# A graph layer on one core: each gather signals the landing of the tile four places back, not seven

## What is computed

```python
k = _decomp(x, nt, w_comp_k, w_basis_k).reshape(n, H, DK)     # q and v likewise
kt = jnp.einsum('nhi,thij->tnhj', k, relation_att)[edge_type, src]
e = (q[dst] * kt).sum(-1) * relation_pri[edge_type] * scale
m = jax.ops.segment_max(e, dst, num_segments=n)
ex = jnp.exp(e - m[dst])
a = ex / jax.ops.segment_sum(ex, dst, num_segments=n)[dst]
vt = jnp.einsum('nhi,thij->tnhj', v, relation_msg)[edge_type, src]
agg = jax.ops.segment_sum(a[..., None] * vt, dst, num_segments=n).reshape(n, DH)
out = relu(_decomp(agg, nt, w_comp_a, w_basis_a) + x @ loop_weight + bias)
result = _layernorm(x + out)
```

## Time and profile before

| | us |
|---|---|
| median of 3 runs (1296.33 to 1299.81) | 1298.27 |
| profiled execution, its span | 1757.2 |
| first gather starts, last gather starts | 199.15, 1641.63 |
| first product on DVE, last | 266.3, 1663.7 |
| busy: PE, DVE, POOL, ACT | 1160.7, 986.6, 881.5, 785.6 |

### The profile page before, as it was taken

How to read it: one execution, slowest core, us unless ns; L and a number is a source line. 1 busy time by engine, 2 the same in 40 slices (tenths; PEclk the granted TensorE clock), 3 DMA queues, 4 the chain that set the end, 5 groups by cost and what they waited for, 6 DMA issues and landing times.

```text
span 1757.2 us, 31429 instructions
## 1 busy us (share of the span) xinstructions
PE 1160.7 (66%) x6730; PEld 962.9 (55%) x6730; DVE 986.6 (56%) x2832; ACT 785.6 (45%) x2217; POOL 881.5 (50%) x915
## 2 busy tenths in 40 slices
PE   8989875657556565566566655566565666656698
PEld 5445434656545554455455554565455565545587
DVE  7877463555445555445555554455554566545677
ACT  4667454444434434443344343443444354434324
POOL 2775354555555554545454545455545554545233
PEclk9999997777677767876777667766777687777699
DMA  8878754555555555545455555555555555555675
GB/s 261 323 289 316 284 172 140 157 148 158 152 159 153 157 151 151 149 141 151 150 163 148 158 152 154 148 160 164 151 162 154 154 168 148 155 150 162 187 242 194
DMA packets 225149, 309.08 MB, mean 176 GB/s; under 512 B 32423, under 2 KB 191119, under 8 KB 217781
## 3 DMA queue, kind: packets, MB, share of 16 engines
q1 hardware_dynamic: 159996, 188.75, 30.6%
q0 software_dynamic: 38880, 106.25, 23.4%
q10 hardware_dynamic: 26088, 12.08, 2.4%
HBM read 139.52 MB, written 58.78 MB: 113 GB/s over the span
## 4 chain that ended last, share of the span: by engine, by line
SPq 34%; issue 31%; PE 12%; DVE 9%; another core or an unknown queue 7%; DMA 2%; DVEq 2%; ACT 1%; POOL 1%; POOLq 0%; ACTq 0%
SPq L1173 27%; PE pb L1900 4%; SPq L1152 2%; PE pb L1923 2%; DVE agg L845 2%; SPq L481 2%; SPq L1170 2%; DVEq L814 2%; DMA kv<-ring 2%; PE pb L2084 1%; SPq L1168 1%; PE pb L2190 1%; PE pb L2028 1%; DVE kv L541 1%
## 5 line engine op out<-in xcount | busy, mean ns | idle before, releaser
L1458 POOL DMA_INDIRECT ring<-table,rows_idx x782 | 745.8, 954 | 736.6 <-SPq L1168 452.5
L2084 PE MATMUL pb<-work,onehot 128*128 128x136 f32 x1664 | 367.5, 358 | 214.1 <-DVE agg L845 152.8
L845 DVE TENSOR_TENSOR agg<-agg,pb 128x136 f32 x832 | 241.8, 291 | 459.9 <-remote 291.8
L2084 PEld LDWEIGHTS pb<-work,onehot 128*128 128x128 f32 x1664 | 307.0, 254 | 242.0 <-issue 210.9
L1650 ACT ACTIVATE work<-pb 128x512 f32<-128x512 f32 x208 | 124.0, 596 | 549.6 <-remote 376.2
L2028 PE MATMUL pb<-q_all,work 128*128 x1664 | 301.0, 340 | 1.3 <-issue 0.8
L2028 PEld LDWEIGHTS pb<-q_all,work 128*128 128x128 f32 x1664 | 280.6, 253 | 7.6 <-issue 4.9
L1637 ACT ACTIVATE work<-lane,neg_lane 128x128 f32<-128x128 f32 x800 | 253.3, 390 | 0.6
L2012 PE MATMUL pb<-ident,onehot 128*128 128x128 f32 x832 | 174.5, 347 | 115.6 <-issue 60.2
L2012 PEld LDWEIGHTS pb<-ident,onehot 128*128 128x128 f32 x832 | 125.4, 180 | 136.0 <-issue 71.3
L686 DVE TENSOR_TENSOR kv<-kv,pb 128x512 f32<-128x512 f32 x208 | 141.5, 680 | 96.6 <-issue 41.7
(11 more groups left out here) (239 smaller groups left out, 1237.2 us busy)
## 6 DMA issues: line engine op xcount, KB each, us to landing
kv<-ring SPq DMA_DIRECT2D x832, 128.0 KB
table<-kv SPq DMA_DIRECT2D x49, 1024.0 KB, 5.2
ring<-table,rows_idx POOLq DMA_INDIRECT x782
kv<-base_rows SPq DMA_DIRECT2D x7, 448.0 KB, 7.6
kv<-in_x_dram SPq DMA_DIRECT2D x8, 384.0 KB, 5.8
seg<-item_bias ACTq DMA_DIRECT2D x48, 64.0 KB
base_rows<-pair ACTq DMA_DIRECT2D x24, 128.0 KB
onehot<-coef_rows SPq DMA_DIRECT2D x3, 1024.0 KB, 5.5
```

The costliest lines, as they stand in the source:

```text
L845: v.tensor_tensor(a, a, PB[banks[i // 2 % len(banks)]][:, (i % 2) * 256:(i % 2) * 256 + W], ALU.add).then_inc(s_added, 1)
L1458: pool.indirect_dma_start(out=ring[:, o:o + 2 * D], out_offset=None, in_=table, in_offset=bass.IndirectOffsetOnAxis(ap=rows_idx[:, t:t + 1 ...
L2084: mm = t_.matmul(PB[banks[k % len(banks)]][:, u * 256:u * 256 + W], onehot[:, o:o + P], wv[:, b % WR, h * 2 + u, :], start=True, stop=True)
```

## The change

The constant AHEAD goes from 7 to 4. It has two uses: the tile that iteration t waits for and announces, and the number of tiles that are announced behind the loop.

```diff
@@ -87,7 +87,7 @@
     REAL = -(-E // P)
     RING = 16
-    AHEAD = 7
+    AHEAD = 4
     TSEMS = 8
     assert AHEAD < TSEMS and RING & (RING - 1) == 0 and GROUPS * G < ITEMS
```

## The result

The changed kernel is slower: median 1345.34 us of 4 runs (1340.1 to 1349.36) against 1298.7 us of the kernel before, ratio 1.0354 with a 95% interval of 1.0322 to 1.0387. The forecast was no change, with a range up to 1318 us.

The account below looks back on a forecast made before the run. The prediction took GpSimd's row of gathers, at 1.254 us each, to bound the timed kernel. From 1298.3 us it took 3 us of gain and added 3 us of cost, giving 1298 us, no change, range 1284 to 1318 us.

Parts of the forecast that it names:

- The bound: Whole timed kernel: GpSimd's row of gathers, 1.254 us each, sets the time, with PE close behind.
- the floor of 1282 to 1294 us: Time of a kernel whose GpSimd never waits; the median stood 4 to 16 us above it.
- Signals come earlier where GpSimd was held: GpSimd's freed wait: landed tiles are announced sooner, loosening the ring; 3 us gain taken, bounds 0 to 16 us.
- rival A: Freed wait, line 1455: the ring was too tight, so the change is faster, about 9 us, 1289 us; chance 0.21.
- The sequencer's lead shrinks: GpSimd's landing wait: gather t can't be handed over before tile t-4 is signalled; 3 us cost, bounds 0 to 39 us.
- limit (3.8 us): Longest time from a gather's start to its signal that delays no even gather; odd ones were allowed 4.3 us.
- rival B: Landing wait before even gathers: landings too late for four in flight; up to 39 us slower, 1318 us at half; chance 0.19.
- The share of late landings: Even gathers at the landing wait: one in twenty late by 0.15 us, 3 us in all.
- The upper bound, 39 us: Most the landing waits could cost: every sixth even gather late by 0.6 us.
- The page's rule: HBM access of 0.2 us on average, 2 us at high load; for the gathers some 300 us cost, given 1 in 100.
- Rival C: PE paces the groups and a cushion in ring and kv hides cost and gain: 1298 us; forecast with C 0.60.
- What the profile after would show: Signs: unheld gathers keep 0.30 us gaps, line 1168 waits stay GpSimd's largest (350 to 550 us), span within 2%.

Follow-up runs that it names:

- the second profile: The kernel before, unchanged, profiled a second time: span 1299.3 us in an execution of 1301.56 us.
- half_rows7: The kernel before (AHEAD = 7) with gathers of 512 bytes instead of 1 KB and copies halved from the third group on: 1279.84 us, ratio 0.9811.
- limit4_signal7: Against the kernel before: iteration t waits for tile t-4's landing but still announces only tile t-7: 1349.73 us, ratio 1.0386.
- load_twice7: The kernel before (AHEAD = 7) with the count load repeated in even iterations; the build dropped the repeat, leaving the same kernel: 1298.89 us, ratio 1.0008.
- two_counts4: The changed kernel (AHEAD = 4) with a second count load and freed wait in even iterations, behind the landing wait: 1393.01 us, ratio 1.0695 to the kernel before.
- half_rows4: The changed kernel (AHEAD = 4) with gathers of 512 bytes instead of 1 KB and copies halved from the third group on: 1298.03 us, ratio 0.9944 to the kernel before.

## Why the prediction was wrong

*The bound.* Right in substance. A row of gathers at 1.254 us paces the timed kernel: the second profile has a mean step of 1.270 us, and half_rows7, with half the bytes, has the pace of 1.254 us itself: 979.3 us for 781 steps, and no wait before a gather is longer than the fixed gap:

```profile
POOL ring L1460 <- issue: 218.4, 717, 0.3
```

It came to 1279.8 us, 2 us under the floor of 1282 to 1294 us, and its tail (105.1 us against 113.9) is shorter as well. The margin to the copies is small, though. The chain of the second profile runs through SyncE's copies more than through the gathers:

```profile
DMA kv<-ring 36%; SPq L1173 10%; DMA ring<-table,rows_idx 8%; PE pb L1900 6%; PE pb L1980 3%; PE pb L1923 3%; POOL ring L1458 3%; PE pb L2190 1%; POOLq L1452 1%; DVE kv L541 1%; DVE agg L845 1%; DVEq L814 1%; PE pb L1909 1%; DVE q_all L954 1%; PE pb L1969 1%
```

On line 1168 SyncE waits 142.2 us for its own copies there, yet it holds the gathers up by 6 us only. After the change the chain runs through the gathers' landings (34%, in the page shown with the result). One statement of this part is refuted: that recording stretches this program by a third. The second profile isn't stretched, and none of the twelve others is.

*Signals come earlier where GpSimd was held: 0 to 3 us of gain.* Not contradicted. limit4_signal7 leaves room for some microseconds, all behind the last gather and none in the row. Before the change only 6 us of GpSimd's waiting on SyncE were left, not 452.5. The 2.0 us of SyncE's waiting for signals, which bounded this term and spoke against rival A, were of the stretched execution: the second profile has 32.9 us, and the changed kernel 158.4.

*The sequencer's lead shrinks: 3 us of cost.* **This is the step that failed.** It measured some 58 us in the row of gathers and 46 us in the time. Mechanism, place and limit (3.8 us) were the right ones and stood there as rival B; the term was mis-sized by a factor of 15. The waits that B asked for are there, and longer than its 0.2 to 0.9 us: up to 2.4 us. Three errors are in it:

1. The share of late landings. I took one in twenty by 0.15 us, from two rows in the tail of the earlier trace rows; it was 114 of 383 by 0.65 us. Those rows came from the first and the last gathers of an execution in which SyncE's slowness kept the copies apart. I had worked out that the timed load is 0.77 in place of 0.52, which the second profile confirms to the digit, and then took the delays of a thinner stretch for it.
2. The upper bound, 39 us, was no bound. It counted late even gathers only and took the worst of twelve rows as the worst there is; the worst of 766 was 6.54 us. It also left out GpSimd's own pauses, below, 10.5 us of the 58.
3. A choice near the end that did no harm, where the evidence (one even row late in six) pointed at the other.

*The page's rule* of 2 us for a memory access at high load (the Trainium skill, DMA: Bandwidth & Descriptors, Latency and other measured facts) is supported in its direction: the median rose by 0.9 us from half to full rows, the 95% point from 4.05 to 4.97 us. No run shows the memory access by itself. Its far end, 1.8 us on every gather, is refuted: its 300 us were six times too much.

*Rival C, PE as the bound with a cushion,* fails. PE's 1.10 us a gather, 87% of the pace, came from the stretched execution, where the granted clock was 0.73. In the second profile the clock is 0.86 and PE is busy 594.6 us for 618 gathers, 0.96 us each, or 77%. And DVE waited for the copies into kv even before, and waits longer now:

```profile
DVE kv L686 <- DMA kv<-ring: 97.5, 75, 3.5
```
```profile
DVE kv L686 <- DMA kv<-ring: 146.7, 90, 3.8
```

(before, second profile; then after). There is no cushion: of the 58 us lost in the gathers all reach the end but the 9 us of the tail and the 1.5 us by which the first gather came sooner.

*What the profile after would show.* The gap of 0.30 us and the step between unheld gathers stayed. The waits on line 1168 did not stay the largest row, and the span did not stay within 2% of 1757 us, but that test was worth little: it was set against an execution that doesn't repeat.

## What to carry to other kernels

Set the number of transfers in flight by the slow tail of their landing times at the full load, plus the work between the wait and the next issue, and not by the median: here 3.58 us at the median lies under the 3.8 us allowed and the change still cost 3.5%, while one more place brought nearly all of it back. A sequencer's lead is what hides its own loads and waits; before it is given up, count how much of them lies behind the wait. And where a profiled execution is a third longer than the timed kernel, take from it the lengths of single instructions at most, no delays of transfers: their load is another one. Even of the lengths not all held here: GpSimd's gathers (954 and 952 ns) and DVE's line 845 (291 and 291 ns) are alike in both profiles, PE's matmuls of line 2084 (358 and 318 ns) are not.

## What was not expected of the hardware

*The same kernel, two profiles.* The span was 1757.2 us in one and 1299.3 us in the other. In the first the steps of SyncE's queue take 0.7 us in stretches, and the mean granted clock is 0.783; in the second it is 0.893, and there and in the twelve profiles of other kernels here the span follows the timed times. It isn't the only long execution: one of the ten of load_twice7 took 1573.1 us, at a mean granted clock of 0.637. Why they were slow, and whether the clock is cause or effect, stays open.

*A pause at every 106th gather.* In the changed kernel iterations 113, 219, 325, 431, 537, 643 and 749 start 1.0 to 2.3 us late (together 13 us), though not for their landings: six of them start 3.35 us after the signal of their iteration and the first 3.42 us after it, where other odd iterations held by a landing need 0.77 us. The first in the timeline of GpSimd:

```profile
345.11 0.94 POOL L1458 DMA_INDIRECT ring<-table,rows_idx  x1 [2.19 <-issue]
```

The same gathers have the same 3.35 us in the kernels with AHEAD = 3, in two_counts4, with more instructions in each iteration, and in half_rows4, with half the bytes. So it goes by gathers and not by instructions or bytes, and some 2.6 us of extra work of the sequencer would explain it. A lead hides it like other work: the seven cost 15.6, 13.3, 7.7, 4.4 and 2.8 us in all with 3, 4, 5, 6 and 7 (one trace each), and nothing in half_rows7. With AHEAD = 7 mainly the last two of the seven are left in the second profile, 2.5 us together; its last:

```profile
1145.18 0.95 POOL L1458 DMA_INDIRECT ring<-table,rows_idx  x1 [2.20 <-issue]
```

What happens in these iterations was not tested. They are 10.5 of the 58 us, and were in none of the terms of the prediction.
